# An embedding, attention and mixture-of-experts tower on one core: entry gathered into three places, squares by halves, routing in pieces along the causal groups

## What is computed

```
emb  = word[ids] + domain[domain_ids] @ proj_w.T + proj_b + type[...] + pos[...]
h    = layernorm(emb) * gamma + beta
h   += magnitude attention(layernorm(h))    # 12 heads of 16: scores = sqrt(re^2 + im^2), softmax
x    = layernorm(h)
x   += causal attention(layernorm(x))       # 12 heads
z    = layernorm(x);  logits = z @ w_g      # 8 experts
best two experts of each token; rank of a token in its expert = how many earlier picks chose it
picks of rank >= capacity (1280) are dropped; weights = softmax over the two
y    = sum over the picks: weight * (gelu(z_slots @ fc_w + fc_b) @ pj_w + pj_b)
out  = h + x + y
```

## Time and profile before

| | us |
|---|---|
| median of 3 runs | 1126.58 (1125.38 to 1136.05) |
| the profiled execution, device time | 1129.93 |
| its span, first to last instruction | 1128.1 |
| PE busy | 934.3 (83%) |
| DVE busy | 665.4 (59%) |
| ACT busy | 673.0 (60%) |
| POOL busy | 464.4 (41%) |

### The profile page before, as it was taken

How to read it: one execution, slowest core, us unless ns; L and a number is a source line. 1 busy time by engine, 2 the same in 40 slices (tenths; PEclk the granted TensorE clock), 3 DMA queues, 4 the chain that set the end, 5 groups by cost and what they waited for, 6 DMA issues and landing times.

```text
span 1128.1 us, 21988 instructions
## 1 busy us (share of the span) xinstructions
PE 934.3 (83%) x7210; PEld 713.2 (63%) x7210; DVE 665.4 (59%) x3058; ACT 673.0 (60%) x1339; POOL 464.4 (41%) x508
## 2 busy tenths in 40 slices
PE   1234888879888979999999999946999999999996
PEld 1222555556555556666666666535888888889896
DVE  1344889879887766676766656374433434433332
ACT  2013888877888877887787778435443443443431
POOL 6666465444000110223222212213476676676654
PEclk7565999999999969999999998655999999999999
DMA  7233232232011100011011012143473455474352
GB/s 196 42 59 54 58 66 38 50 60 37 19 29 24 35 2 1 2 34 34 2 34 34 4 32 62 34 82 34 88 110 68 89 110 75 78 114 74 53 56 28
DMA packets 64259, 59.23 MB, mean 53 GB/s; under 512 B 17534, under 2 KB 55328, under 8 KB 64160
## 3 DMA queue, kind: packets, MB, share of 16 engines
q0 software_dynamic: 26112, 27.89, 18.0%
q1 hardware_dynamic: 38048, 30.12, 10.3%
HBM read 35.28 MB, written 16.39 MB: 46 GB/s over the span
## 4 chain that ended last, share of the span: by engine, by line
PE 55%; DVE 14%; ACT 11%; issue 7%; POOL 6%; DMA 4%; SPq 2%; ACTq 0%; POOLq 0%; DVEq 0%
PE ps_scores L724 13%; PE ps_ring L716 9%; PE ps_ring L965 7%; PE ps_ring L724 6%; POOL got L547 4%; PE ps_scores L965 4%; PE ps_scores L839 4%; ACT square L1061 3%; PE ps_ctx L856 3%; PE ps_scores L842 3%; SPq L458 2%; DVE probs L1329 2%; DMA got<-place_rows,id_now 2%; PE ps_ring L796 1%; ACT prob_t L1054 1%
## 5 line engine op out<-in xcount | busy, mean ns | idle before, releaser
L598 POOL DMA_INDIRECT out<-z_t,slots_now x80 | 135.3, 1692 | 102.1 <-DVE z_t L1624 83.0
L1168 ACT ACTIVATE probs<-ps_scores,fc_bias 128x512 f32<-128x512 f32 (+1 forms) x144 | 88.3, 617 | 146.9 <-PE ps_scores L724 143.7
L1054 ACT ACTIVATE prob_t<-ps_ring 128x512 f32<-128x512 f32 x192 | 113.8, 595 | 34.9 <-PE ps_ring L716 32.9
L716 PE MATMUL ps_ring<-ident,probs 128*128 128x128 f32 x768 | 127.8, 292 | 5.6 <-DVE x_hi L1222 2.5
L1061 ACT ACTIVATE square<-ps_scores 128x1024 f32<-128x1024 f32 x96 | 98.3, 1024 | 45.5 <-PE ps_scores L839 44.3
L1329 DVE CUSTOM_DVE_ANT_0 probs<-ps_scores,causal 128x128 f32<-128x128 f32 x384 | 88.8, 286 | 58.4 <-PE ps_scores L842 58.0
L1077 ACT ACTIVATE probs<-probs,neg_max 128x128 f32<-128x128 f32 x384 | 120.7, 395 | 3.6 <-DVE neg_max L1329 3.6
L965 PE MATMUL ps_ring<-work,probs 128*128 128x192 f32 x672 | 115.9, 328 | 5.6 <-ACT probs L1168 5.4
L1323 DVE CUSTOM_DVE_ANT_0 probs<-square 128x128 f32<-128x128 f32 x384 | 89.0, 286 | 46.2 <-ACT square L1061 43.1
L965 PEld LDWEIGHTS ps_ring<-work,probs 128*128 128x128 f32 x672 | 109.2, 190 | 9.4 <-issue 9.4
L724 PE MATMUL ps_scores<-x_hi,fc_hi 128*128 128x512 f32 (+1 forms) x288 | 105.1, 370 | 7.4 <-DVE x_hi L1608 4.8
(11 more groups left out here) (211 smaller groups left out, 2207.3 us busy)
## 6 DMA issues: line engine op xcount, KB each, us to landing
k<-k_signed SPq DMA_DIRECT2D x192, 32.0 KB
work<-pj_w SPq DMA_DIRECT2D x8, 576.0 KB, 4.4
token_in<-xin SPq DMA_DIRECT2D x8, 384.0 KB, 3.5
out<-resid SPq DMA_DIRECT2D x8, 384.0 KB, 4.3
vals<-fc_w SPq DMA_DIRECT2D x8, 384.0 KB, 3.4
vals<-fc_w SPq DMA_DIRECT2D x16, 192.0 KB, 4.2
out<-z_t,slots_now POOLq DMA_INDIRECT x80, 3.6
token_in<-xin SPq DMA_DIRECT2D x8, 128.0 KB, 4.3
```

The lines of the kernel that those rows point to most:

```text
L598: gp.indirect_dma_start(out[:, :], bass.IndirectOffsetOnAxis(slots_now[:, u, 1, t:t + 1], 0), slot_y[:, o, :], None, compute_op=ALU.add).t ...
L716: return pe.transpose(dst, src, ident[0:n, 0:n])
L1054: sc.activation(prob_t[:, s % 2, :, :], src.rearrange("p (h q) -> p h q", h=4), ACT.Exp if p is mag else ACT.Copy).then_inc(ring_free[i], 1)
L1168: sc.activation(hidden[:, c % 2, f_, 0:128 * nt], ps_scores[:, i, 0:128 * nt], ACT.Gelu, bias=fc_bias[:, e, f_:f_ + 1]).then_inc(gelu_done ...
```

## The change

- **Entry.** Only group 0's rows go to three places (`got` and two in `square`), by plain gathers that do not wait for each other, and DVE adds them (two adds of 128x768). `id_now` has two halves, so the word gathers of a group no longer wait for the group before. The loads of the causal weights wait until group 0's rows have landed.
- **Later embeddings.** `EMBED_LATE` moves the embedding of group 1 and 2 by 9 slots, 3 by 5, 4 by 2. Group 1's projections move to slots 9 to 13 of pass 0; group 0's values come after its projections. POOL's roots move to its slots 4 and 12 (4 and 6 for groups 0 and 1), ahead of that slot's gather.
- **Keys.** Group 0's keys are turned with 8 DMAs over all three blocks instead of 24.
- **Squares.** ACT squares two heads at a time, two instructions a job, each freeing its half of the scores.
- **Routing.** Each causal group is routed behind its logits, in pieces of one a slot (`ROUTE`): choices, rank, slots, low one-hots, high one-hots, parts, weights, map. Rank and map are two more fills of the ring. Group 15 is routed in two batches of two sequences (`LAST_ROUTE`). Second picks of an expert are numbered down from its last slot, so that one running count over the groups will do. The map is summed in SBUF (`slot_map`). The scans, the ring of 16 turns, ACT's scaling and the matmuls of L904 go.
- **End of the passes.** `LAST_LAGS` grow by a slot from ctx to logits. The first expert's weights are split in four quarters, a slot each.

The diff, cut to its core:

```diff
-XT_SLOT = {"mag": (0, 1), "cau": (1, 2)}
+XT_SLOT = {"cau": (1, 2)}
+EMBED_LATE = (0, 9, 9, 5, 2, 0, 0, 0)
+EARLY_PROJ, EARLY_VALUE = {1: (9, 10, 10, 11, 12, 13)}, {0: (14, 15), 1: (14, 15)}
...
-LAST_LAGS = {"ctx": 4, "ctxT": 5, "out": 7, "scale": 7, "norm": 9, "zT": 10, "keep": 11, "logits": 12}
+LAST_LAGS = {"ctx": 5, "ctxT": 6, "out": 8, "scale": 8, "norm": 10, "zT": 11, "keep": 11, "logits": 13}
...
+ROUTE = {"rank": 1, "slots": 2, "low": 3, "high": 4, "parts": 5, "weights": 6, "map": 7}
+LAST_ROUTE = ({"rank": 2, "slots": 4, "low": 4, "high": 5, "parts": 5, "weights": 5},
+              {"rank": 1, "slots": 1, "low": 1, "high": 1, "parts": 1, "weights": 2, "map": 2})
...
-            for g in range(GROUPS):
+            sp.wait_ge(keys_signed, BLOCKS)
+            for quarter, part in product(range(4), range(2)):
+                sp.dma_start(k_of[0][to:to + HEAD_DIM, :, 1, :, :].rearrange("p b s k -> p b (s k)"),
+                             k_signed[of:of + HEAD_DIM, :, :]).then_inc(first_turned, 16)
+            for g in range(1, GROUPS):
...
             def gather_step(g, slot):
                 if slot == 0:
-                    if g > 0:
-                        pool.wait_ge(dom_got, 16 * GROUP * g)
                     if g > 1:
+                        pool.wait_ge(dom_got, 16 * GROUP * (g - 1))
                         pool.wait_ge(mag.named("emb_affine0"), g)
...
+                    if g == 0:
+                        gather(apart_from_word[0], place_rows, g, slot - 4, place_got, 2, ALU.bypass)
...
             def embedding_norm(p, g, slot):
-                first, second = (2, 5) if p < 0 else (5, 11)
+                first, second = (4, 6) if g < 2 else (4, 12)
...
             def squares(g, j):
-                act.wait_ge(mag.scores_full, 2 * (JOBS * g + j) + 2)
-                sc.activation(square[:, j % 2, :, :, :]..., ps_scores[:, :, 0:256], ACT.Square
-                              ).then_inc(mag.scores_free, 2)
+                for pair in range(2):
+                    act.wait_ge(mag.scores_full, 2 * (JOBS * g + j) + pair + 1)
+                    h = slice(2 * pair, 2 * pair + 2)
+                    sc.activation(square[:, j % 2, h, :, :]..., ps_scores[:, h, 0:256], ACT.Square
+                                  ).then_inc(mag.scores_free, 1)
...
+                elif kind == "rank":
+                    first, end = BATCHES(number)[s]
+                    width = TOPK * EXPERTS
+                    pe.wait_ge(hot_ready, batch_no(number, s))
+                    tiles = lambda a, b: dst[:, width * (a - first):width * (b - first)]
+                    pe.matmul(tiles(first, end), below[:, :], hots[:, 1 + first:1 + end, :], start=True, stop=False,
+                              skip_group_check=True)
+                    for t in range(-1, end - 1):
+                        to = max(t + 1, first)
+                        last = pe.matmul(tiles(to, end), ones_b[:, :],
+                                         hots[:, 1 + t:2 + t, :].to_broadcast([128, end - to, width]),
+                                         start=False, stop=(t == end - 2), skip_group_check=True)
+                    if number == LAST and end == GROUP:
+                        for t in range(1 + GROUP):
+                            last = pe.matmul(dst[:, 256:256 + width], ones_b[:, :], hots[:, t, :],
+                                             start=(t == 0), stop=(t == GROUP), skip_group_check=True)
+                elif kind == "map":
+                    pe.wait_ge(lows_made, batch_no(number, s))
+                    pe.wait_ge(parts_made, batch_no(number, s))
+                    for k in range(TOPK):
+                        for t in range(GROUP):
+                            last = pe.matmul(dst[:, 2 * HIGH * k:2 * HIGH * (k + 1)], low_hot[:, TOPK * t + k, :],
+                                             high_part[:, TOPK * t + k, :, :], start=(t == 0), stop=(t == GROUP - 1),
+                                             skip_group_check=True)
...
+            def mark_choices(no, b):
+                done = batch_no(no, b)
+                now, pairs, tt = tiles_of(no, b)
+                dve.wait_ge(cau.named("ordered"), tt.stop)
+                ve.tensor_tensor(gap[:, 0, tt], best[:, tt, 1], best[:, tt, 0], ALU.subtract).then_inc(gap_ready, 1)
+                ve.tensor_copy(chosen[:, now, :], best_at[:, tt, 0:TOPK]).then_inc(chosen_made, 1)
+                dve.wait_ge(number_made, 1)
+                dve.wait_ge(chosen_made, done)
+                pick = chosen[:, :, :].rearrange("p t k -> p (t k)")[:, pairs]
+                n_pairs = pairs.stop - pairs.start
+                ve.tensor_tensor(hots[:, 1 + now.start:1 + now.stop, :].rearrange("p t (k e) -> p (t k) e", e=EXPERTS),
+                                 number[:, 0:EXPERTS].unsqueeze(1).to_broadcast([128, n_pairs, EXPERTS]),
+                                 pick.unsqueeze(2).to_broadcast([128, n_pairs, EXPERTS]),
+                                 ALU.is_equal).then_inc(hot_ready, 1)
+            def take_ranks(no, b, free, n, src):
+                done = batch_no(no, b)
+                now, pairs, tt = tiles_of(no, b)
+                nt, width = now.stop - now.start, TOPK * EXPERTS
+                dve.wait_ge(hot_ready, done)
+                if no == LAST and now.stop == GROUP:
+                    ve.tensor_tensor(used[:, :].rearrange("p (e n) -> p e n", e=EXPERTS),
+                                     in_expert.unsqueeze(1).to_broadcast([128, EXPERTS, CAP_TILES]),
+                                     src[:, 256:256 + EXPERTS].unsqueeze(2).to_broadcast([128, EXPERTS, CAP_TILES]),
+                                     ALU.is_ge)
+                ve.tensor_tensor(rank_hot[:, pairs, :].rearrange("p (t k) e -> p t (k e)", k=TOPK),
+                                 src[:, 0:nt * width].rearrange("p (t w) -> p t w", w=width),
+                                 hots[:, 1 + now.start:1 + now.stop, :], ALU.mult).then_inc(free, 1)
+                if no < LAST:
+                    with nc.allow_low_precision(reason="counts below 33"):
+                        ve.tensor_reduce(hot_sum[:, :], hots[:, :, :].rearrange("p t w -> p w t"), AX.X, ALU.add
+                                         ).then_inc(sums_made, 1)
+                dve.wait_ge(free, n + 2)
+                ve.tensor_reduce(rank[:, :, :].rearrange("p t k -> p (t k)")[:, pairs], rank_hot[:, pairs, :], AX.X,
+                                 ALU.add).then_inc(ranked, 1)
+                if no < LAST:
+                    dve.wait_ge(sums_made, 2 * done - 1)
+                    ve.tensor_copy(hots[:, 0, :], hot_sum[:, :]).then_inc(sums_made, 1)
+            def route_piece(what, no, b):
+                done = batch_no(no, b)
+                now, pairs, tt = tiles_of(no, b)
+                n_pairs = pairs.stop - pairs.start
+                if what == "slots":
+                    dve.wait_ge(ranked, done)
+                    far = over[:, now, :]
+                    ve.tensor_scalar(far, rank[:, now, :], float(CAP), None, ALU.is_ge)
+                    ve.scalar_tensor_tensor(out=slot_f[:, now, 0], in0=chosen[:, now, 0], scalar=float(CAP),
+                                            in1=rank[:, now, 0], op0=ALU.mult, op1=ALU.add)
+                    step(ve.scalar_tensor_tensor(out=slot_f[:, now, 1], in0=chosen[:, now, 1], scalar=float(CAP),
+                                                 in1=rank[:, now, 1], op0=ALU.mult, op1=ALU.subtract))
+                    ve.scalar_tensor_tensor(out=slot_f[:, now, 0], in0=far[:, :, 0], scalar=2.0 * SLOTS,
+                                            in1=slot_f[:, now, 0], op0=ALU.mult, op1=ALU.add)
+                    ve.tensor_scalar(far[:, :, 1], far[:, :, 1], 2.0 * SLOTS, float(CAP - 1), ALU.mult, ALU.add
+                                     ).then_inc(route, 1)
+                    count[0] += 1
+                    dve.wait_ge(route, count[0])
+                    step(ve.tensor_tensor(slot_f[:, now, 1], slot_f[:, now, 1], far[:, :, 1], ALU.add))
+                    slots = slot_f[:, :, :].rearrange("p t k -> p (t k)")[:, pairs]
+                    if no > GROUPS:
+                        dve.wait_ge(map_added, no - GROUPS)
+                    step(ve.tensor_scalar(at_low[:, pairs], slots, -(LOW - 1) / 2, TO_LOW, ALU.add, ALU.add))
+                    step(ve.tensor_scalar(at_high[:, pairs], at_low[:, pairs], -TO_LOW, None, ALU.add))
+                    ve.tensor_tensor(at_low[:, pairs], slots, at_high[:, pairs], ALU.subtract).then_inc(slots_made, 1)
+                elif what == "low":
+                    dve.wait_ge(slots_made, done)
+                    ve.tensor_tensor(low_hot[:, pairs, :], number.unsqueeze(1).to_broadcast([128, n_pairs, LOW]),
+                                     at_low[:, pairs].unsqueeze(2).to_broadcast([128, n_pairs, LOW]), ALU.is_equal
+                                     ).then_inc(lows_made, 1)
```

(20 more changed lines are left out.)

328 lines of the change are left out of this document (180 added, 148 removed).

## The result

The changed kernel took 1118.85 us (median of 20 runs, 1111.85 to 1125.34) beside 1126.02 us before (20 runs): a ratio of 0.9925, 95% interval 0.9899 to 0.9951, so 8.4 us off by the ratio and 7.2 by the medians. I forecast 22.5 us off and 1104. The sign holds, and the time lies inside my range; the size is a third of the forecast.

The account below looks back on a forecast made before the run. No single engine was taken as the bound: idle engines at entry, no leader in magnitude passes, PE in causal passes, then a serial stretch before the experts. -32 + 24 - 14.5 = -22.5 us, from 1126.6 to 1104; range 1084 to 1127.

Parts of the forecast that it names:

- Entry to `xn`: Group 0's embedding at the start: plain place gathers and two DVE adds bring `xn` at 37.7 instead of 47.6, 10 us.
- Keys and pass 0: First magnitude pass: keys landed at 55.3, jobs of 1.3 to 1.6 us instead of 2.49, group 2 35 us ahead.
- POOL's chain, 8 us back: Magnitude passes: roots ahead of gathers lengthen POOL's chain to 22.3 us; groups 3 to 5 lose 2 to 4 each.
- Rival B: Entry's lead is eaten by POOL's chain, slow key turns or a late pass 1: 12 of 32 left, 1124 us; chance 0.15.
- Squares by halves 5 us off: Magnitude passes: ACT's half squares shorten DVE's waits, 5 us off, between a loss of 7 and a gain of 20.
- The entry as a whole: Entry and magnitude passes together: 35 - 8 + 5 = 32 us off, range 24 to 40.
- the sign that I had named for a wrong forecast: At the first causal scores: the forecast is wrong if they come less than 24 us earlier.
- Routing, 24 us on: Causal passes: DVE's routing pieces add 4.2 us in each of passes 9 to 13 and 1.4 in 14 and 15.
- not above 85: Causal passes: a sign of the forecast was DVE above 85% busy in a pass of about 43 instead of 39 us.
- The end, 14.5 off: After the last logits: first expert gather 16.8 us earlier, less 2.3 charged for colliding loads; range 10 to 18.
- The sum: Whole kernel: -32 + 24 - 14.5 = -22.5 us, giving 1104 us from the median.

Follow-up runs that it names:

- narrow_keys: The change's entry half alone, POOL's second root ahead of the last two domain gathers, group 0's keys turned in 24 DMAs instead of eight: 0.9756 of before, 1097.4 us.
- entry_only: The kernel before with the change's entry half alone (embeddings, key turns, squares, root order), routing all at the end: 0.9818 of before, 1108.8 us.
- route_only: The kernel before with the other half alone: routing in pieces along with the causal groups, later last lags, first weights by quarters: 1.0106 of before, 1141.0 us.
- dve_load: Entry half alone, POOL's second root ahead of two domain gathers, plus ten idle 128x512 DVE operations in each of six causal passes: 0.9947 of before, 1120.2 us.
- whole_squares: The changed kernel with a job's squares in one ACT instruction again instead of two halves: 1.0006 of the kernel before, 1128.9 us.

## Why the prediction was wrong in size

**Entry to `xn`: right.** 10 us off was forecast, 9.6 measured; the two adds ended at 28.8, 1.3 us later than I put them, since the weights' split ended late.

**Keys and pass 0, forecast 14 us too early: the first step that failed.** Keys were on hand at 59.5 instead of 55.3: they were signed 1.9 us later, and after the eight issues (5.5 us) came 4.5 of landing, not 2.6. And a job took 2.06 us, not 1.3 to 1.6. I had PE and ACT work side by side on the two halves. In the rows each half goes round by itself: PE 0.6 (half of 1.24), ACT 0.6 (its mean), and the two handovers between them, by difference 0.85 together, and that round is the period of 2.06. The third job's scores came at 63.7 (57 forecast), group 2's moments at 95.4 (81): from the first scores to these moments the pass took 35.8 us, and I had counted 25.7. The width of the key turns is not the reason (narrow_keys); that a job's period is, is read from the rows, and no run shortens it. At group 2's `xn` in slot 5 of pass 1 the lead was 21.0 us (117.4 against 138.4), where I forecast 35. These 14 us are most of the 16 that the profile lacks at the first causal scores.

**"POOL's chain, 8 us back": too small, the second step that failed.** The chain is right as to its place: DVE waits for POOL's root behind four domain gathers. It was 22.1 us in group 2 (95.35 to 117.44), I said 22.3, so its wait of 4.9 us was inside my 35. But for the groups behind it I spread the price as 2 to 4 us over groups 3 to 5 and counted the wait alone. It fell in group 5 with 4.1 us, while in groups 3 and 4 DVE's own moments were late; and behind each of the two waits PE ran at half clock. The lead fell from 21.0 us at slot 5 of pass 1 to 10.3 at the first maxima of pass 4 (237.4 and 247.7). Moving the root by two gathers, groups 2 and 5 together, gave back 12 to 17 us in the timed runs and 7 to 13 in the profiles. Rival B named the mechanism ("group 2's chain on POOL ... a late pass 1 leave 12 of the 32") at 0.15; with the entry at 16 to 20 the outcome lies between the forecast and B.

**"Squares by halves 5 us off": too small.** They gave 9 to 10, twice the term, with an interval of 5 to 13, and most of it in later passes and not in pass 0, where I looked for a good part. This error made up for a part of the two above.

**The entry as a whole.** 32 was forecast; the runs give 20.5 (entry_only), the profile 16, and the sign that I had named for a wrong forecast came up: the first causal scores were less than 24 us earlier. With the root moved the first causal maxima are 29.5 us ahead (382.1 and 411.6), within the 24 to 40 that I gave.

**Routing, 24 us on: the size right, its working only half.** From the second causal group's first maxima to the last logits the changed kernel loses 20.8 us (20.6 ahead, then 0.2 behind), route_only 28.7; to the last maxima it is 21.3 and 24.5. That 24 lies between is in part luck. I counted five full passes, 9 to 13, and pass 9 has no piece in it: there were four. That DVE's time holds up PE was the mechanism, and dve_load shows it for most of the price. But full-clock passes cost 3 to 4 us and not 4.2, and the last group 3.1 where I said 1.4; what makes up the sum is a clock of 0.92 to 0.96, which no term had: the four passes together are 16.7 us longer than before. DVE was 76% busy in a routed pass (33.2 of 43.4), not above 85: it need not be full to hold up PE, since every slot has its own chain. The pieces also took 5.5 us and not 7.05: parts cost 0.38 + 0.52, where I had 1.4. Here the estimate of 0.9 us that I made from the Trainium skill (VectorE: DVE Perf Modes, What auto-detection actually checks) was right, and my scaling from an f32 row was not.

**The end, 14.5 off: right in size behind the last logits, with a cost ahead of them that I put too low.** The slot table came 10.3 us after the last logits (11.5 forecast), the first gather at 12.4 (15.5 forecast), and it landed 2.3 slower (2.3 charged). 17.5 us came off by the first expert layer, 1.6 went back among the experts: 15.9. The seventh group's pieces, the last group's first batch and its later lags lie between the last maxima and the last logits; I charged 1.5 us for the last two. That stretch took 44.7 us, and 45.3 before, as if it cost nothing. But its length goes with the clock. Before, the changed kernel, then entry_only and narrow_keys, which have the old end (columns of the earlier trace rows):

```profile
699.40:744.70 45.30, 39.51 (x238) 26.12 (x236) 19.07 (x74) 19.04 (x43) 13.11 (x29) 0.65 0.10 26
...
700.20:744.90 44.70, 36.33 (x261) 25.00 (x260) 28.24 (x124) 18.72 (x45) 12.86 (x26) 0.77 0.18 44
...
673.30:712.40 39.10, 31.50 (x237) 21.30 (x235) 18.88 (x74) 18.76 (x43) 13.11 (x29) 0.85 0.11 30
...
667.10:713.05 45.95, 40.55 (x238) 26.68 (x236) 19.03 (x74) 19.08 (x43) 13.10 (x29) 0.62 0.09 25
```

At a clock as low as in the profile before (0.65), route_only needs 49.5 us (0.67) for it, and whole_squares 50.8 (0.63) where narrow_keys has 45.9: 4 to 5 us more at a like clock. So the profiles of before and after hide a cost of that size, and the end by itself gains nearer 11 or 12 than 15.9. That agrees with the timed route_only, 12 us on with 24.5 lost up to the last maxima.

The Trainium skill (DMA: Bandwidth & Descriptors, SWDGE vs HWDGE vs iDMA) says that inside a DMA engine GpSimd's and SyncE's queues are served in turn, and that the engine changes between them only at the bounds of packets of up to 64 descriptors. My prediction took single descriptors, and twice the time, 3 to 4 us more, was my estimate and not the page's. Here 7.1 against 5.25 us is 1.4 times: a slowing is there, as turns would give, and it is smaller than I estimated.

**The sum.** By the profiles: 16.4 ahead at the first causal maxima, 4.2 more in the first causal pass, which the profile before ran at a clock of 0.86, then 20.8 lost and 15.9 gained at the end, 15.7 in all. By the timed halves it is -20.5 + 12 = -8.5, where I had -32 + 9.5 = -22.5. So 11.5 of the missing 14 us are the entry's, and 2.5 those of middle and end. The entry fell short by a late pass 0 and by a chain on POOL whose waits the clock made dearer. The terms of the middle and of the end make a loss together; read by halves, the sum would have pointed to entry_only.

## What to carry to other kernels

Split a change with several parts into the halves that can ship alone, and forecast each: here one half gained 1.8%, the other lost 1.1%, and one slot number was worth another 1.2%. Work moved from a serial tail into a loop is not free because its engine is only 70% busy there: if that engine holds the one that bounds, half of its time comes out as time even with a fifth to a quarter of that engine idle, and the clock can add to that (here 5 of 6.4 us in the passes that lost clock). Look for the first long wait of the engine whose clock can fall: its removal can pay more than its length. And compare stretches of two profiles only with the clock of each beside them, since here one stretch of unchanged instructions took 39 or 46 us.

## What was not expected of the hardware

Stretches in which PE was busy 2.9 and 4.4 of 8 us were followed by a granted clock of 0.70 and 0.58 over the next 8. In the causal passes much less did it: 3.28 us busy of 4, and then about 7 us at 0.50. But entry_only had 3.05 and 3.33 of 4 at 483 to 491 us with the clock at 1.00, so what sets it stays open. Three routed passes of one profile at 0.92 and 0.96 next to one at 1.00 with the same instructions show that it is not fixed for the program either. Whether idle matmuls in PE's waits would hold the clock was not tried.

One-source bf16 work in SBUF on DVE: 640 elements in 0.38 us, where 512 of f32 took 0.49.
